# Group and instance sums through TensorE in pairs, maxima by a diagonal, the frame on GpSimd, and a new order of queues in a fused double convolution block

## The chip, the cores and the metric

The kernel runs on one core of one Trainium2 chip. The metric is the device time of one execution in microseconds; the median of three runs is taken. Five engines work side by side, each with an instruction queue of its own that runs strictly in order: TensorE (PE, matmuls), VectorE (DVE), ScalarE (ACT), GpSimd (POOL) and SyncE (SP), which here issues every transfer. They meet through semaphores. A queue whose first instruction waits holds back all that stands behind it.

## The reference, cut to what matters

The input x has the shape 8 x 32 x 128 x 128 (images, channels, rows, columns), fp32. Two residual blocks follow each other:

```python
x = x + _L0_conv_ref(_gn(x), L0_conv_weight, L0_conv_bias)
x = x + _L1_conv_ref(_gn(x), L1_conv_weight1, L1_conv_weight2)
```

`_gn` is a group norm with 16 groups of 2 channels, without weights. `_L0_conv_ref` rounds its input and its weights to integers from -127 to 127 (`q = round(t * 127 / max|t|)`, the maximum taken over the whole tensor of all images), convolves them 3x3, scales back and adds a bias. `_L1_conv_ref` is twice a convolution whose kernel is a weighted sum of fixed basis patterns, each followed by an instance norm and a leaky ReLU with slope 0.2:

```python
h = _instnorm_lrelu(_disco_conv(image, weight1))
return _instnorm_lrelu(_disco_conv(h, weight2))
```

At this size only five taps of that kernel are not zero: the centre and its four neighbours. Every norm needs a mean and a variance over pixels that lie on several partitions.

## The kernel before, in words

**Layout.** The 128 partitions are 4 bands of rows (quads) times 32 channels. An image in that layout is 128 x 4096 fp32, 2 MB. PSUM has 8 banks, used as two sets of four: every convolution of an image is done in two halves, g=0 into set 0 (banks 0 to 3) and g=1 into set 1 (banks 4 to 7). While one set is filled, the other is drained.

**Start.** All images are loaded one by one (`xa`), their group norms computed, the normalised x written out by GpSimd (`gn_x`, L658) and its absolute maximum taken by VectorE (`x_max`, L827). The maximum over the nine parts (L854) is taken over the partitions by GpSimd's `partition_all_reduce` (L673); L584 does the same for the weights. From it VectorE makes the factors of the rounding (L857 to L864, `quant_known`). `to_low` turns a piece of x (a quarter of an image) into int16 (ScalarE L530, GpSimd L691), `to_q` turns that into fp16 in the padded tile `qpad` or `c2one` (VectorE L874 for images 0 and 1, GpSimd L698 for the others).

**Three convolutions.** `quantised(b)`, v=0 (L1025), is the 3x3 convolution in fp16; VectorE adds its result to x plus bias (`x1_add`, L883) in the tile `x1_of(b)`, one of five (`LIVE`). `half(1, b, g)` (L1062) is half of the first five-tap convolution in fp32, with weights that `scale_taps` has multiplied by the norm's factor, and with a frame round the image that holds the mean (`frame`, L798 to L801), so that the norm need not be applied to the data. ScalarE copies it from PSUM to `hpad` (`take(1, t, g, n)`, L503) and applies norm and ReLU there in three steps (`make_h`, L516). `half(2, t, g)` is the second five-tap convolution, taken by ScalarE to `c2one` or `slot(4)` (`take(2, t, g, n)`), then normed in four pieces (`norm_out`, L524), added to x1 (`output`, GpSimd L704, VectorE L918 for the last two images) and stored. Each of the convolutions needs the rows of neighbouring partitions, which SyncE copies (`q_edges`, `x1_edges`, `h_edges`).

**The order.** `ORDER` sets TensorE's: after three opening entries the loop over t=0 to 5 runs `quantised(t+2)`, conv 1 of image t+1 and conv 2 of image t; then conv 1 of image 7 and conv 2 of images 6 and 7. A half may start when both pairs of banks of its set have been taken (`wait_set`). Each other engine has its own hand-written list over t, so all waits below come from these lists. `load_xb(b)` fetches x again for the addition, in four pieces of 0.5 MB, and `add_bias(b)` (ScalarE, L509) waits for all four (`xb_in`).

**Statistics.** VectorE reads each bank (`conv_stats`, L903) or the rows of x1 (`x1_stats`, L893) and joins them to one mean and variance per partition (`own_stat`). To sum over the partitions of a group or channel there are two ways. By DRAM: SyncE writes 128 x 2 numbers (`write_share`, L381), waits, and reads them back spread (`read_share`, L388 and L391). By TensorE: VectorE multiplies the numbers by a mask (`spread`), one small matmul with a matrix of zeros and ones sums them (`gather`, L979; for x L1082), and VectorE reads PSUM. `BY_PE` names the three cases of 24 that go by TensorE; `GATHERS` says after which tap the gather stands. `group_moments` (L789) makes the moments from either, and GpSimd makes scale and shift from them (`scale_of`, L619 and L622; `normalise`, L628; `scale_taps`, L638).

## Time and profile before

| what | us |
|---|---|
| median of 3 runs | 432.95 |
| lowest and highest | 431.23, 433.69 |
| the profiled execution | 430.53 |
| its span | 428.7 |
| busy: TensorE, VectorE, ScalarE, GpSimd | 258.9, 249.6, 214.2, 183.9 |
| TensorE's mean granted clock, of full speed | 0.908 |

The profile is of one execution. Busy times are sums of an engine's records. The chain of waits is followed back from the last instruction to whatever released it, and so says what set the end; "issue" in it is time in which the engine waited for nothing that the profile shows. In all rows PE is TensorE, DVE VectorE, ACT ScalarE, POOL GpSimd and SPq the queue of SyncE; L12 is line 12 of the program.

### The profile page before, as it was taken

The page shows a single profiled execution, that of the slowest core. Times are in us where ns is not written, and L with a number is a line of the kernel's source. Part 1 is how long each engine was busy: PE and PEld are TensorE (multiplying, and loading weights), DVE is VectorE, ACT ScalarE, POOL GpSimd, SP SyncE. Part 2 cuts the span into 40 slices and gives each one's busy share as a digit, 9 for nine tenths or more (in the row PEclk, how much of TensorE's full clock was granted, in tenths as well). Part 3 has the DMA queues.
Part 4 walks back from the last instruction along what each step waited for, and adds up shares of the span by engine and source line. Part 5 has one row for each costly group of instructions (what it writes and reads, how often), then busy time and mean ns, then how long its engine had stood idle before and what let it go on. Part 6 is the DMA issues. An engine that isn't in the chain of part 4 may idle for free.

```text
span 428.7 us, 14659 instructions
## 1 busy us (share of the span) xinstructions
PE 258.9 (60%) x6718; PEld 138.9 (32%) x6718; DVE 249.6 (58%) x418; ACT 214.2 (50%) x189; POOL 183.9 (43%) x220
## 2 busy tenths in 40 slices
PE   0011010373877977896896697459885994979700
PEld 0000000321443542462443253124442551655500
DVE  1838998169739717934860771348616853553264
ACT  1089981630321645492546440915474461676453
POOL 0298963196100905564824650638244063081000
PEclk9999999998898996998999699678996999798955
DMA  8999309602811906343824395328353141333066
GB/s 262 395 426 405 148 1 241 151 6 72 215 12 31 225 6 167 82 112 85 221 55 100 102 283 171 100 62 235 63 101 100 33 126 12 103 116 96 2 196 196
DMA packets 96513, 59.11 MB, mean 138 GB/s; under 512 B 20164, under 2 KB 95268, under 8 KB 95268
## 3 DMA queue, kind: packets, MB, share of 16 engines
q1 hardware_dynamic: 96452, 58.19, 47.7%
q8 instruction: 52, 0.85, 1.0%
q14 instruction: 9, 0.07, 0.1%
HBM read 36.41 MB, written 16.80 MB: 124 GB/s over the span
## 4 chain that ended last, share of the span: by engine, by line
DMA 33%; DVE 24%; POOL 15%; PE 9%; issue 7%; SPq 6%; ACT 5%; DVEq 0%; POOLq 0%; ACTq 0%
DMA stat_c<-own_stat_c 10%; DMA share_c<-stat_c 9%; DMA stat_x<-own_stat_x 9%; DVE amax L827 7%; PE ring L1062 6%; DVE bn_c L903 6%; SPq L388 3%; DVE bn_x L893 3%; DMA hpad<-w_dram 2%; ACT hpad L516 2%; DVE live L883 2%; DMA share_x<-stat_x 2%; POOL hpad L691 2%; POOL xs L691 2%; POOL qpad L698 2%
## 5 line engine op out<-in xcount | busy, mean ns | idle before, releaser
L1062 PE MATMUL ring<-hpad,w12t 32*32 32x512 f32 x2560 | 98.3, 619 | 16.2 <-ACT hpad L503 8.8
L903 DVE BATCH_NORM_STATS2 bn_c<-ring 128x6 f32<-128x512 f32 x128 | 79.1, 681 | 32.4 <-PE ring L1062 32.2
L1025 PE MATMUL ring<-qpad,w0t 64*32 64x512 f16 x1344 | 54.4, 488 | 39.4 <-ACT c2one L503 16.9
L1062 PEld LDWEIGHTS ring<-hpad,w12t 32*32 32x32 f32 x2560 | 54.8, 104 | 53.0 <-issue 28.6
L1062 PE MATMUL ring<-xs,w1s 32*32 32x512 f32 x1280 | 48.7, 632 | 8.9 <-ACT xs L503 5.3
L503 ACT COPY hpad<-ring 128x1024 f32<-128x1024 f32 x32 | 31.7, 1010 | 42.3 <-DVE bn_c L903 42.1
L619 POOL TENSOR_SCALAR var_eps<-moments_c 128x1 f32<-128x1 f32 x16 | 3.0, 191 | 107.8 <-DVE moments_c L789 107.8
L1062 PE MATMUL ring<-live,w1s 32*32 32x512 f32 x1280 | 46.4, 597 | 3.1 <-issue 3.1
L1025 PEld LDWEIGHTS ring<-qpad,w0t 64*32 64x32 f16 x1344 | 21.9, 114 | 74.2 <-ACT c2one L503 20.4
L789 DVE BATCH_NORM_AGGREGATE moments_x<-share_x 128x2 f32<-128x24 f32 x7 | 1.8, 264 | 66.6 <-DMA share_x<-stat_x 66.6
L516 ACT ACTIVATE hpad<-hpad,params 128x1536 f32<-128x1536 f32 (+1 forms) x24 | 35.0, 1523 | 10.2 <-POOL params L628 10.2
L1062 PEld LDWEIGHTS ring<-xs,w1s 32*32 32x32 f32 x1280 | 25.8, 105 | 30.6 <-issue 16.1
L503 ACT COPY xs<-ring 128x1024 f32<-128x1024 f32 x16 | 16.2, 1015 | 37.7 <-DVE bn_c L903 37.7
L503 ACT COPY c2one<-ring 128x1024 f32<-128x1024 f32 x16 | 16.3, 1020 | 32.6 <-DVE bn_c L903 32.5
L619 POOL TENSOR_SCALAR var_eps<-moments_x 128x1 f32<-128x1 f32 x8 | 2.0, 251 | 70.0 <-DVE moments_x L789 70.0
L1062 PEld LDWEIGHTS ring<-live,w1s 32*32 32x32 f32 x1280 | 24.4, 103 | 23.2 <-issue 14.5
L509 ACT ACTIVATE xs<-xs,single 128x1024 f32<-128x1024 f32 x16 | 17.1, 1146 | 25.4 <-DMA xs<-xb_dram 25.4
L691 POOL TENSOR_SCALAR xs<-xs,q_scale,q_shift 128x1024 int16<-128x1024 f32 x22 | 26.3, 1195 | 1.8
L524 ACT ACTIVATE c2one<-c2one,params 128x1024 f32<-128x1024 f32 x16 | 18.6, 1231 | 15.5 <-POOL params L628 15.5
L827 DVE TENSOR_REDUCE amax<-live 128x1 f32<-128x4096 f32 x5 | 22.0, 4393 | 6.9 <-POOL live L658 6.9
L460 ACT ACTIVATE qpad<-xs 128x4096 f16<-128x4096 f32 x4 | 14.4, 3608 | 17.4 <-DMA xs<-xa_dram 17.4
L883 DVE SCALAR_TENSOR_TENSOR live<-ring,single,live 128x512 f32<-128x512 f32 x32 | 21.5, 739 | 2.5 <-PE ring L1025 2.5
(107 smaller groups left out, 383.5 us busy)
## 6 DMA issues: line engine op xcount, KB each, us to landing
xs<-xa_dram SPq DMA_DIRECT2D x8, 2048.0 KB, 10.4
live<-xb_dram SPq DMA_DIRECT2D x16, 512.0 KB, 6.9
xs<-xb_dram SPq DMA_DIRECT2D x16, 512.0 KB, 7.0
out_dram<-live SPq DMA_DIRECT2D x16, 512.0 KB, 4.9
out_dram<-xs SPq DMA_DIRECT2D x16, 512.0 KB, 5.1
hpad<-xa_dram SPq DMA_DIRECT2D x1, 2048.0 KB, 8.4
live<-live SPq DMA_DIRECT2D x8, 192.0 KB, 2.8
xs<-xs SPq DMA_DIRECT2D x8, 192.0 KB, 3.2
```

The lines of the kernel that those rows point to most:

```text
L388: sp.dma_start(share[s][f:P:2, :, 1:3], of.unsqueeze(0).to_broadcast([QUADS, C // 2, GN_MEMBERS, 2])).then_inc(shared[s], 16)
L460: nc.scalar.activation(junk, grid(x_first(b)), ACT.Identity, scale=1.0 / (SUM_ROOT * COLS), accum_out=own_x[:, b, 1:2]).then_inc(x_meaned, 1)
L503: nc.scalar.copy(to, pair_of(g, n)).then_inc(taken[v], 1)
L509: nc.scalar.activation(x, x, ACT.Identity, bias=bias[:]).then_inc(biased, 1)
L516: nc.scalar.activation(rows, rows, ACT.Prelu, bias=param(shift["c1"], t), scale=param(scale["c1"], t), alpha=SLOPE).then_inc(h_ready, 1)
L524: nc.scalar.activation(y, y, ACT.Prelu, bias=param(shift["c2"], t), scale=param(scale["c2"], t), alpha=SLOPE).then_inc(out_norm, 1)
L691: nc.gpsimd.tensor_scalar(low_of(b, n), piece(source, n), q_scale[:, b:b + 1], q_shift[:, b:b + 1], ALU.mult, ALU.add).then_inc(low_pool, 1)
L827: nc.vector.tensor_reduce(amax[:, n:n + 1], gn_tile(b)[:, c0:c1], AX.X, ALU.max, apply_absolute_value=True).then_inc(max_done, 1)
L883: ins = nc.vector.scalar_tensor_tensor(x, grid(ring[:, bank_of(g, 2 * i + p), :]), dequant[:], x, ALU.mult, ALU.add)
L903: ins = nc.vector.bn_stats(bn[f"c{v}"][:, QUADS * g + k, :], ring[:, bank_of(g, k), :])
L1025: ins = nc.tensor.matmul(ring[C * c:C * (c + 1), bank_of(g, 2 * i + p), :].rearrange("p (y x) -> p y x", x=IMG), w0t[q, tap, :], q_of(b)[q ...
L1062: ins = nc.tensor.matmul(ring[C * c:C * (c + 1), bank_of(g, r), :].rearrange("p (y x) -> p y x", x=IMG), w, window(v, b, r, c, g, dy, dx), ...
```

## The change

What it does:

- The sums of x1 for all images and of c1 (the first five-tap convolution) for all images go by TensorE. For images in the loop, x1(t+2) and c1(t+1) are gathered in one stop, after the third tap of `half(2, t, 1)`, into a bank of set 0. In the title's words "second convolution" is this one: the quantised one is the first. Of c2 the last two images go by TensorE; images 0 to 5 stay with DRAM.
- Both maxima over the partitions are taken by a diagonal: VectorE multiplies an identity matrix (loaded from DRAM as a new input) by the 128 maxima, TensorE multiplies by a matrix of ones, and VectorE reduces the row in PSUM. `qmul` falls away, its factor is joined into the next step.
- `frame` moves from VectorE to GpSimd, behind `scale_taps`.
- In the conversions before the loop ScalarE makes two pieces of image 0 and two of image 1, GpSimd the rest; `add_bias(0)` stands ahead of them.
- The lists of SyncE, ScalarE, GpSimd and VectorE are put in another order. `load_xb(t+3)` and `add_bias(t+3)` are split in two for t from 1 to 4 and stand earlier; in the tail some outputs change engine.

The order on SyncE in iteration t=2, before:

```order
L372 DMA live<-xb_dram 128x8x128 [waits stored0]
L372 DMA live<-xb_dram 128x8x128 x3
L347 DMA hpad<-hpad 96x128 [waits h_ready]
L348 DMA hpad<-hpad 96x128
L381 DMA stat_c<-own_stat_c 4x32x2 [waits stat_step_c2]
L391 DMA share_c<-stat_c 128x4x2 [waits written_c2]
```

and after:

```order
L391 DMA stat_c<-own_stat_c 4x32x2 [waits stat_step_c2]
L386 DMA live<-xb_dram 128x8x128 [waits stored0]
L386 DMA live<-xb_dram 128x8x128
L395 DMA share_c<-stat_c 128x4x2 [waits written_c2]
L360 DMA hpad<-hpad 96x128 [waits h_ready]
L361 DMA hpad<-hpad 96x128
L386 DMA live<-xb_dram 128x8x128 [waits stored0]
L386 DMA live<-xb_dram 128x8x128
```

The sums of c2 went ahead of the load, and the load is cut in two round `h_edges`; the two trips of x1 and c1 that stood later in the iteration are gone.

The order on ScalarE in iteration t=2, before (L516 is `make_h`, L503 a take, L524 `norm_out`, L509 `add_bias`):

```order
L516 ACTIVATE hpad<-hpad,params 128x4x2x128 [waits conv1_taken,norm_ready_c1]
L516 ACTIVATE hpad<-hpad,params 128x4x3x128 x2
L503 COPY hpad<-ring 128x2x4x128 [waits conv2_done,conv1_counted]
L503 COPY hpad<-ring 128x2x4x128 [waits conv1_counted]
L524 ACTIVATE xs<-xs,params 128x1024 [waits conv2_taken,norm_ready_c2]
L524 ACTIVATE xs<-xs,params 128x1024 x3
L503 COPY hpad<-ring 128x2x4x128 [waits conv1_counted] x2
L509 ACTIVATE live<-live,single 128x8x128 [waits xb_in5]
L509 ACTIVATE live<-live,single 128x8x128 x3
```

and after (the same in this order: L515, L502, L523, L508):

```order
L515 ACTIVATE hpad<-hpad,params 128x4x2x128 [waits conv1_taken,norm_ready_c1]
L515 ACTIVATE hpad<-hpad,params 128x4x3x128 x2
L508 ACTIVATE live<-live,single 128x8x128 [waits xb_in5]
L508 ACTIVATE live<-live,single 128x8x128
L502 COPY hpad<-ring 128x2x4x128 [waits conv2_done,conv1_counted]
L502 COPY hpad<-ring 128x2x4x128 [waits conv1_counted]
L508 ACTIVATE live<-live,single 128x8x128 [waits xb_in5]
L508 ACTIVATE live<-live,single 128x8x128
L523 ACTIVATE xs<-xs,params 128x1024 [waits conv2_taken,norm_ready_c2]
L502 COPY hpad<-ring 128x2x4x128 [waits conv1_counted] x2
L523 ACTIVATE xs<-xs,params 128x1024 x3
```

`add_bias`, with its wait for the load, moved from the end of the row to right behind `make_h`, ahead of the takes.

The order on GpSimd where the maximum of x is taken, before:

```order
L658 TENSOR_SCALAR c2one<-hpad,gn_scale,gn_shift 128x2048 [waits max_done,norm_ready_x]
L673 ISA
L673 ISA single<-single 128x1 [waits amax_step]
L676 MEMSET c2one 128x2x130 [waits max_done]
L677 MEMSET c2one 128x32x2
L691 ISA
L691 TENSOR_SCALAR hpad<-xs,q_scale,q_shift 128x1024 [waits quant_known]
```

and after:

```order
L681 TENSOR_SCALAR c2one<-hpad,gn_scale,gn_shift 128x2048 [waits max_done,norm_ready_x]
L696 MEMSET c2one 128x2x130 [waits max_done]
L697 MEMSET c2one 128x32x2
L711 TENSOR_SCALAR hpad<-xs,q_scale,q_shift 128x1024 [waits quant_known]
L711 TENSOR_SCALAR hpad<-xs,q_scale,q_shift 128x1024 x3
```

The all-reduce and both plain ISA rows round it are gone.

In the diff, cut to its core, a line of "..." marks what is left out:

```diff
+GATHERS = {(0, 1, 0): (6, [("x1", 0)]), (1, 0, 1): (3, [("x1", 1)]), (1, 1, 0): (4, [("c1", 0)]),
+           (2, B - 2, 0): (4, [("c1", B - 1)]), (2, B - 1, 0): (4, [("c2", B - 2)])}
+for _t in range(B - 2):
+    GATHERS[2, _t, 1] = (3, [("x1", _t + 2), ("c1", _t + 1)])
+LAST_GATHER = ("c2", B - 1)
...
             for t in range(B - 2):
+                if t >= 1:
+                    write_share(t - 1)
+                if t >= 1 and t + 3 < B:
+                    load_xb(t + 3, (0, 1))
+                if t >= 1:
+                    read_share(t - 1)
+                h_edges(t)
+                if t >= 1 and t + 3 < B:
+                    load_xb(t + 3, (2, 3))
+                x1_edges(t + 2)
...
+            add_bias(0)
 
             act.wait_ge(quant_known, 1)
...
                 for n in range(3):
                     make_h(t, n)
+                if t >= 1 and t + 3 < B:
+                    add_bias(t + 3, (0, 1))
                 take(1, t + 1, 0, 0)
                 take(1, t + 1, 0, 1)
+                if t >= 1 and t + 3 < B:
+                    add_bias(t + 3, (2, 3))
                 if t >= 1:
-                    for n in range(QUADS):
-                        norm_out(t - 1, n)
+                    norm_out(t - 1, 0)
                 take(1, t + 1, 1, 0)
                 take(1, t + 1, 1, 1)
-                if t + 3 < B:
-                    add_bias(t + 3)
+                if t >= 1:
+                    for n in range(1, QUADS):
+                        norm_out(t - 1, n)
...
-            pool.wait_ge(amax_step, 1)
-            nc.gpsimd.partition_all_reduce(sx[:], amax1[:], P, ABSMAX).then_inc(sx_done, 1)
...
+            def max_of_all(all_of, of, n, bank):
+
+                nc.vector.tensor_scalar(diagonal, eye, of, None, ALU.mult).then_inc(max_diagonal, 1)
+                dve.wait_ge(max_shared, n + 1)
+                return nc.vector.tensor_reduce(all_of, ring[:, bank, 0:P], AX.X, ALU.max)
...
             own_of("x1", 0)
-            x1_add(1, 0)
             group_moments("x1", 0)
-            frame(0)
...
                 conv_stats(1, t + 1, 1)
+                conv_stats(2, t, 0)
                 group_moments("x1", b)
-                frame(b)
-                conv_stats(2, t, 0)
                 group_moments("c1", t + 1)
...
+            def share_max(n, bank):
+                pe.wait_ge(max_diagonal, n + 1)
+                nc.tensor.matmul(ring[:, bank, 0:P], ones, diagonal, start=True, stop=True).then_inc(max_shared, 1)
```

## Rows read from the trace of the kernel before

**Rows 1.** The page: busy time, then the chain by line.

```profile
PE 258.9 (60%) x6718; PEld 138.9 (32%) x6718; DVE 249.6 (58%) x418; ACT 214.2 (50%) x189; POOL 183.9 (43%) x220
...
DMA stat_c<-own_stat_c 10%; DMA share_c<-stat_c 9%; DMA stat_x<-own_stat_x 9%; DVE amax L827 7%; PE ring L1062 6%; DVE bn_c L903 6%; SPq L388 3%; DVE bn_x L893 3%; DMA hpad<-w_dram 2%; ACT hpad L516 2%; DVE live L883 2%; DMA share_x<-stat_x 2%; POOL hpad L691 2%; POOL xs L691 2%; POOL qpad L698 2%
```

**Rows 2.** Chain of waits at the start: start us, length us, what.

```profile
12.97 4.80 issue
...
40.99 0.61 PE ring L1082 x2
...
74.59 2.59 issue
...
78.52 6.08 issue
```

**Rows 3.** The same chain inside iterations t=2 and t=3.

```profile
205.46 4.38 ACT hpad L516 x3
...
225.76 5.74 DMA stat_x<-own_stat_x
...
233.74 4.27 DMA stat_c<-own_stat_c
```

**Rows 4.** Groups of instructions: out<-in, shapes, xcount, busy us, mean ns, idle before.

```profile
L903 DVE BATCH_NORM_STATS2 bn_c<-ring 128x6 f32<-128x512 f32 x128 | 79.1, 681 | 32.4 <-PE ring L1062 32.2
...
L503 ACT COPY hpad<-ring 128x1024 f32<-128x1024 f32 x32 | 31.7, 1010 | 42.3 <-DVE bn_c L903 42.1
...
L883 DVE SCALAR_TENSOR_TENSOR live<-ring,single,live 128x512 f32<-128x512 f32 x32 | 21.5, 739 | 2.5 <-PE ring L1025 2.5
...
L524 ACT ACTIVATE c2one<-c2one,params 128x1024 f32<-128x1024 f32 x16 | 18.6, 1231 | 15.5 <-POOL params L628 15.5
L704 POOL TENSOR_TENSOR xs<-xs,c2one 128x1024 f32<-128x1024 f32 x8 | 17.3, 2178 | 2.7 <-ACT c2one L524 2.7
...
L509 ACT ACTIVATE live<-live,single 128x1024 f32<-128x1024 f32 x16 | 17.0, 1142 | 0.0
...
L798 DVE TENSOR_SCALAR live<-zeros,moments_x 128x64 f32<-128x64 f32 x4 | 1.1, 284 | 0.1
```

**Rows 5.** Timeline of TensorE: start us, length us, instruction, xcount, idle before.

```profile
87.98 1.48 PE L1025 MATMUL ring<-qpad,w0t 64*32 64x512 f16 x24 [8.83 <-DVE qpad L874]
...
123.22 2.80 PE L1025 MATMUL ring<-qpad,w0t 64*32 64x512 f16 x95
...
163.36 8.04 PE L1025 MATMUL ring<-qpad,w0t 64*32 64x512 f16 x192 [4.86 <-ACT c2one L503]
...
326.64 8.30 PE L1025 MATMUL ring<-qpad,w0t 64*32 64x512 f16 x192 [5.87 <-ACT c2one L503]
...
364.27 12.99 PE L1062 MATMUL ring<-xs,w1s 32*32 32x512 f32 x311 [5.32 <-ACT xs L503]
```

**Rows 6.** Stretches: busy (xcount) by engine, then PEclk, DMA share, GB/s.

```profile
228.30:234.00 5.70, 5.55 (x160) 2.88 (x160) 0.00 (x0) 4.11 (x4) 1.28 (x1) 1.00 0.48 95
...
274.00:281.50 7.50, 7.27 (x160) 3.43 (x160) 0.00 (x0) 4.23 (x5) 1.39 (x1) 0.74 0.34 74
```

**Rows 7.** Timeline of SyncE's queue, iteration t=2.

```profile
204.97 4.14 SPq L372 DMA_DIRECT2D live<-xb_dram  x4
```

**Rows 8.** The line of load_xb, and the page's issues of stores.

```profile
DMA to landing us min/median/max: 4.3/7.0/9.4
...
out_dram<-live SPq DMA_DIRECT2D x16, 512.0 KB, 4.9
```

**Rows 9.** Waits of TensorE: us in total, times, longest.

```profile
PE ring L1062 <- issue: 10.5, 14, 1.6
```

**Rows 10.** Chain of waits in the tail.

```profile
396.72 3.84 DMA stat_c<-own_stat_c
...
400.57 3.56 DMA share_c<-stat_c
...
418.15 3.50 DVE xs L918 x3
```

More of the change, by code:

```diff
@@ L154, in slot @@
             return xs[:, n * COLS:(n + 1) * COLS]
+        eye, ones, diagonal = (flat(hpad[0])[:, n * P:(n + 1) * P] for n in range(3))
         last_x = flat(hpad[1])[:, 0:COLS]
@@ L308, in low_pool_count @@
         def low_pool_count(b, n):
-            return 2 + 4 * (b - 1) + n
+            return 4 + 4 * (b - 2) + n
         def shares(s, n):
-            return sum((s, m) not in BY_PE for m in range(n + 1))
+            return sum((s, m) not in GATHER_SET for m in range(n + 1))
         block = ctx.enter_context(nc.Block())
@@ L525, in norm_out @@
                                      alpha=SLOPE).then_inc(out_norm, 1)
+            add_bias(0)
             act.wait_ge(quant_known, 1)
-            for n in (0, 1):
-                nc.scalar.activation(low_of(0, n), piece(x_first(0), n), ACT.Identity,
-                                     bias=q_shift[:, 0:1], scale=q_scale[:, 0:1]).then_inc(low_act, 1)
-            add_bias(0)
+            for b in range(2):
+                for n in (0, 1):
+                    nc.scalar.activation(low_of(b, n), piece(x_first(b), n), ACT.Identity,
+                                         bias=q_shift[:, b:b + 1], scale=q_scale[:, b:b + 1]).then_inc(low_act, 1)
             add_bias(1)
@@ L561, in _ @@
             take(1, z, 0, 1)
-            for n in range(QUADS):
+            for n in range(2):
                 norm_out(t - 1, n)
@@ L565, in _ @@
             take(1, z, 1, 1)
-            take(2, t, 0, 0)
             for n in range(3):
                 make_h(z, n)
+            take(2, t, 0, 0)
             take(2, t, 0, 1)
+            for n in range(2, QUADS):
+                norm_out(t - 1, n)
             for n in range(2):
                 take(2, t, 1, n)
+            for n in range(QUADS):
+                norm_out(t, n)
             take(2, z, 0, 0)
             take(2, z, 0, 1)
-            for n in range(QUADS):
-                norm_out(t, n)
             take(2, z, 1, 0)
@@ L708, in _ @@
             pool.wait_ge(quant_known, 1)
[L709 to L712 removed]
+            for b in range(2):
+                for n in (3, 2):
+                    to_low(b, n)
+            for n in range(4):
+                to_low(2, n)
             pool.wait_ge(q_dve, 4)
@@ L716, in _ @@
             zero_bands(hpad[1]).then_inc(h_border, 1)
-            for n in range(4):
-                to_low(2, n)
-            for n in range(4):
-                to_q(2, n)
+            to_q(2, 0)
+            to_q(2, 1)
             scale_taps(0)
-            scale_taps(1)
-            normalise("c1", 0)
+            frame(0)
+            to_q(2, 2)
+            to_q(2, 3)
             for t in range(B - 2):
+                scale_taps(t + 1)
+                frame(t + 1)
+                normalise("c1", t)
                 if t + 3 < B:
@@ L731, in _ @@
                     normalise("c2", t - 1)
[L732 removed]
+                    for n in range(QUADS):
                         output(t - 1, n)
[L734 to L743 removed]
+            t, z = B - 2, B - 1
+            scale_taps(z)
+            frame(z)
+            normalise("c1", t)
+            normalise("c2", t - 1)
+            output(t - 1, 0)
+            output(t - 1, 1)
+            normalise("c1", z)
+            output(t - 1, 2)
+            output(t - 1, 3)
+            normalise("c2", t)
+            output(t, 2)
+            output(t, 3)
+            normalise("c2", z)
         @block.vector
@@ L927, in _ @@
             own_of("x1", 0)
-            x1_add(1, 0)
             group_moments("x1", 0)
-            frame(0)
-            x1_add(1, 1)
+            for g in range(2):
+                x1_add(1, g)
             for g in range(2):
@@ L962, in _ @@
             conv_stats(1, z, 1)
+            group_moments("c1", z)
             conv_stats(2, t, 0)
-            group_moments("c1", z)
             conv_stats(2, t, 1)
+            group_moments("c2", t)
             conv_stats(2, z, 0)
-            group_moments("c2", t)
-            for n in range(QUADS):
-                output(t, n)
+            output(t, 0)
+            output(t, 1)
             conv_stats(2, z, 1)
```

263 lines of the change are left out of this document (120 added, 143 removed).

## The prediction

> **What bounds the kernel now.** I read the chain of waits first: no engine is busy more than 60% of the span, and the largest links of the chain are not arithmetic but transfers of a few hundred sums to DRAM and back [rows 1]. Then the same chain inside one iteration of the loop over t: a write of x1's sums takes 5.74 us, c1's write 4.27, with a read behind each, all issued by SyncE in one row, and only behind them come conv statistics, `make_h` and the next convolution [rows 3]. Then TensorE's own timeline: `quantised(3)` starts at 163.36, `quantised(7)` at 326.64, the last `half(1, 7)` at 364.27 [rows 5]. So four iterations take 163.3 us, 40.8 each, and the next 37.6. What must TensorE itself do in one? Half of a fp32 convolution of 160 records takes 5.55 us at a granted clock of 1.00 [rows 6], `quantised` 2.80 for one of its two halves [rows 5]: 4 x 5.55 + 2 x 2.80 = 27.8 us. 13 us of each iteration are waits. The start is the third view: between the maximum over all (DVE L854) and the first conversion on GpSimd lie 2.59 us, the all-reduce, and 6.08 us in which GpSimd waits for nothing the profile shows; a similar hole of 4.80 us follows the first all-reduce [rows 2].
>
> **The change part by part.** Times below are against the profiled execution (span 428.7).
>
> *Maxima.* One all-reduce goes; in its place stand a `tensor_scalar` of 128x128, one matmul of 128x128 and a `tensor_reduce` from PSUM. The nearest matmul pair over 128 partitions took 0.61 us [rows 2]; three small VectorE steps at 0.28 [rows 4] and the hand-overs make about 1.5 us, between 1.1 and 2.5. Two scalar steps fall out before `quant_known`. 74.59 + 1.5 + 0.6 gives `quant_known` at 76.7, against 78.5. The holes of 6.08 and 4.80 us: in the instruction order an ISA row stands at L673 and another at L691, right where the 6.08 us lie, and likewise at L584 and L593; in the new order both pairs are gone but for one at the very start. I take the 6.08 as gone (bounds 0 and 6.1). The early 4.80 is worth less, since later sums on ScalarE and the loads of x pace that stretch: 2.9 us, less 0.4 us for one more load in front: 2.5 (bounds 0 and 4.8). Now the cover: `add_bias(0)` stands ahead of ScalarE's conversions. Its four pieces take 4 x 1.14 [rows 4]; its load lands about 7 us after the issue [rows 8], before `quant_known`, so it costs about nothing (up to 1 us if it lands late). The conversions of image 1 are split over ScalarE and GpSimd. The last cast of image 0, and with it TensorE's first matmul at 87.98 [rows 5], comes at about 78.6: **9.4 us** gained.
>
> *Order at the start.* `group_moments("x1", 0)` now stands ahead of `x1_add(1, 0)`, 4 adds of 0.67 [rows 4]: 1.9 us. The moments of x1(1) stood behind a round trip by DRAM; now they come inside `half(1, 0, 1)`, and VectorE's next statistics no longer queue behind the transfer: 4.4 us at `quantised(2)`. Iteration t=0 then needs 2.8 (rest of `quantised`), two convolutions, 1.3 where the takes stand behind `make_h`, and the pauses below: 28.4 against 32.5, 4.1 us. Sum 9.4 + 1.9 + 4.4 + 4.1 = **19.8**: `quantised(3)` starts at 143.6.
>
> *Pair of gathers.* x1(t+2) and c1(t+1) are summed in one stop after tap 3 of `half(2, t, 1)`: two matmul pairs of 0.61, in all 0.7 to 1.3 us on TensorE per iteration. The gather waits for the spreads (VectorE, about 2 us earlier) and for `take(2, t, 0, 0)`, since it writes into that bank. Behind it stand two taps of the convolution and everything else of TensorE. The moments follow about 1.8 us later, just as the convolution ends, so `quantised(t+3)` loses at most 0.3.
>
> *Frame on GpSimd.* On VectorE the three fills cost 0.28 each [rows 4], and VectorE is no bound, so their leaving gains nothing by itself. On GpSimd I take 1.1 us with their mutual waits; the trace has no such fill on GpSimd, and an add of 1024 columns takes 2.18 there [rows 4], so 0.8 to 6.5 for the three. `scale_taps` (1.4) and `frame` end 2.3 us after `quantised` starts; `half(1, t+1)` needs them 5.6 after it. Hidden, with 3.3 us to spare, except before `half(1, 7)`, where no `quantised` stands between: 1.1 us there.
>
> *Loads and ScalarE.* Here lies the new wait, and it decides the sum. Count from T, the start of `quantised(t+2)`, t from 1 to 4. VectorE has c2's aggregate at T+3.0, SyncE writes it, and issues two pieces of `load_xb(t+3)`, for which the last store of t-2 must have landed, 4.9 us after its issue [rows 8], near T. `read_share` comes at 7.7, `h_edges` until 9.9, then the other two pieces at about 1.03 each [rows 7], the last one at 10.9. A piece lands 4.3 to 7.0 us after issue [rows 8]; with two in a row I take 5: T+16. But `add_bias(t+3, (0, 1))` waits for all four (`xb_in` at 64) and stands on ScalarE ahead of `take(1, t+1, 0)`. ScalarE is ready for it at T+8 (takes until 3.65, then `make_h` of 4.38 [rows 3]). So: add_bias 16.0 to 18.3, two takes of 1.01 [rows 4] to 20.4, while TensorE, finished with `half(1, t+1)` at 16.9, waits 3.5 us for them. Then two pieces to 22.7, one `norm_out` of 1.23 to 23.9, two takes to 26.0, three `norm_out` to 29.7, `take(2, t, 0, 0)` at 30.75: only now may the gather run. TensorE started `half(2, t, 0)` at 20.4; whether the idle time lowers its clock (a half took 7.27 at 0.74 and 5.55 at 1.00 [rows 6]) doesn't matter, as the gather waits for 30.75 anyway. Two gathers and two taps: 30.75 + 0.7 + 2.2 = 33.7. A second loop gives the same: `norm_out` of piece 3 feeds GpSimd's add of 2.18, the store, its landing, the loads: 33.8. To this I add TensorE's pauses with no releaser, 10.5 us in 16 fp32 convolutions [rows 9], 0.65 each, 1.3 per iteration: **35.0 us**, 4 x 35.0 = 140 against 163.3, **23.3** gained. With a piece that lands in 4.3 us the iteration is 34.3, in 7.0 it is 37.
>
> *Iteration t=5* has no load: 27.8, gathers 0.7, hand-overs 1.5, pauses 1.3 and the wait for the frame 1.1: 32.4 against 37.6, **5.2**.
>
> *Tail.* From `half(1, 7, 0)`: 11.1, then four taps of `half(2, 6, 0)` and the gather of c1(7), moments at 16.4; GpSimd 1.1, `make_h` 4.4, `take(2, 6, 0)` 2.0: `half(2, 7, 0)` starts at 24.0, ends 29.7, its second half 35.3; statistics, spread, gather, moments 4.1; GpSimd 1.1; first `norm_out` 1.25 and four adds (three took 3.50 [rows 10]) 46.7; store and close 6: 53, with pauses 54.3, against 428.7 - 364.3 = 64.4: **10.1**. The round trip of c2(6), 3.84 + 3.56 [rows 10], is the bulk of it. VectorE adds two pieces of image 6 while GpSimd adds others. The Trainium skill (SBUF — State Buffer, on the shared port pair) says that a VectorE instruction with two SBUF inputs blocks against a GpSimd one that reads SBUF; by it one such add may wait 2.18, and with 0.9 us of slack ahead of the last statistics the tail would be 1.3 longer. No row of before has the two side by side; my sum leaves it out.
>
> Sum: 19.8 + 23.3 + 5.2 + 10.1 = 58.4, span 370.3. Around the span lie 1.8 us, and the median is 2.4 above the profiled execution: 370.3 + 1.8 + 2.4 = **375**.
>
> **The rivals.** *A: the iteration doesn't shorten.* The store, load, `add_bias`, take, `norm_out` loop has so much jitter (landings up to 9.4 [rows 8], an issue of SyncE ahead of each) that iterations 1 to 4 stay at 40.8. Only start and end gain: 375 + 23 = 398. For it: two loops of equal length meet in one queue. Against: it needs a landing at T+22.
>
> *B: TensorE bound.* If the loads land before ScalarE asks (T+8), the iteration is 30: 375 - 20 = 355. Against: two pieces are issued only after 9.9. For it: if SyncE issues two pieces quicker than four in a row and TensorE's clock stays up, part of this comes true.
>
> *C: the hole of 6.08 us stays*, because it isn't the all-reduce that brings it, and the change doesn't do there what it says: 375 + 6 = 381, inside the range.
>
> *D: slower.* TensorE is held in its queue at the pair of gathers by ScalarE, which is held by a load. This decides from the point at which the five iterations give back the 35 us of start and tail and 2 more: 7.5 us over 40, hence a gather at T+44 and a landing at T+30 in every iteration. 35.0 + 13 = 48 each, 375 + 5 x 13 = 440. The nearest row is the slowest landing, 9.4, which is far from it.
>
> **How the numbers follow.** Forecast with its bounds (start gains 14 to 22, iteration 34 to 37, tail 8 to 12), C within it: 0.70, 366 to 388. A and what lies between, 388 to 400: 0.14. B in part or whole, 354 to 366: 0.12. D 0.02; the rest, a gain that almost vanishes, 0.02. The range 358 to 400 leaves out part of B, D and the rest. Faster by over 0.5% (about what a measurement of this kernel can tell from no change) 0.96, within it 0.02, slower 0.02.
>
> **What would show it.** Right: no hole on GpSimd after `quant_known`; x1 and c1 sums gone from the chain; `quantised` at 35 us intervals; ScalarE waiting some 8 us for the xb load after `make_h`, TensorE waiting for `hpad` takes before `half(2, t, 0)`. Wrong: an interval near 30 with ScalarE never waiting for a load (B), or near 40 (A); a hole that stays (C).

## The result, and the profile after

The changed kernel takes 397.79 us (median of four runs, 394.1 to 398.43) against 432.09 us of the kernel before, measured again beside it: a ratio of 0.9187 [0.912, 0.9253]. The forecast was 375.0 with a range from 358 to 400. So the sign and the range held, and the forecast itself was 23 us too low. The profiled execution has a span of 396.6 us against a predicted 370.3. Where a median doesn't answer exactly to its ratio below, the ratio leaves out runs that were disturbed.

The page of the kernel after: busy times, the chain by engine and by line, and the two groups of `add_bias`.

```profile
PE 254.8 (64%) x6752; PEld 138.1 (35%) x6752; DVE 252.6 (64%) x407; ACT 214.7 (54%) x191; POOL 194.8 (49%) x242
...
DMA 26%; PE 18%; DVE 16%; ACT 15%; SPq 10%; POOL 8%; issue 4%; DVEq 0%; POOLq 0%; ACTq 0%
PE ring L1086 14%; DMA xs<-xb_dram 8%; DMA xs<-xa_dram 8%; DMA live<-xb_dram 6%; DVE amax L851 5%; POOL live L724 4%; DVE bn_c L929 4%; SPq L386 4%; SPq L360 3%; ACT hpad L502 3%; ACT xs L508 3%; DMA stat_c<-own_stat_c 2%; PE ring L1049 2%;
...
L508 ACT ACTIVATE xs<-xs,single 128x1024 f32<-128x1024 f32 x16 | 17.3, 1141 | 56.7 <-DMA xs<-xb_dram 56.7
...
L508 ACT ACTIVATE live<-live,single 128x1024 f32<-128x1024 f32 x16 | 17.3, 1144 | 28.1 <-DMA live<-xb_dram 28.1
```

Beside [rows 1] and [rows 4]: TensorE, VectorE and ScalarE do about the work they did before, GpSimd 11 us more. The other group of `add_bias` in the kernel before has one wait, at the start:

```profile
L509 ACT ACTIVATE xs<-xs,single 128x1024 f32<-128x1024 f32 x16 | 17.1, 1146 | 25.4 <-DMA xs<-xb_dram 25.4
```

So ScalarE never waited in front of `add_bias` in the loop over t, and now it waits 84.8 us in front of it in all: 27.7 at the start, where the kernel before waited 25.4, and 57.1 in the loop. Transfers still hold 26% of the chain, but other ones: 14% are the loads of x for the addition, 2% are left of the writes of c2's sums.

TensorE's timeline, to set beside [rows 5]: the starts of the `quantised` convolutions from image 0 on, then `half(1, 7, 0)`; between them the longest wait of an iteration and the longest pause.

```profile
81.25 1.48 PE L1049 MATMUL ring<-qpad,w0t 64*32 64x512 f16 x24 [2.35 <-DVE qpad L900]
...
117.27 5.41 PE L1049 MATMUL ring<-qpad,w0t 64*32 64x512 f16 x192
...
156.92 5.42 PE L1049 MATMUL ring<-qpad,w0t 64*32 64x512 f16 x192
...
183.24 10.45 PE L1086 MATMUL ring<-hpad,w12t 32*32 32x512 f32 x256 [7.72 <-ACT hpad L502]
...
210.18 8.21 PE L1086 MATMUL ring<-xs,w1s 32*32 32x512 f32 x185 [3.10 <-issue]
...
231.78 5.71 PE L1049 MATMUL ring<-qpad,w0t 64*32 64x512 f16 x192
...
271.00 5.41 PE L1049 MATMUL ring<-qpad,w0t 64*32 64x512 f16 x192
...
308.15 5.62 PE L1049 MATMUL ring<-qpad,w0t 64*32 64x512 f16 x192
...
341.40 4.44 PE L1086 MATMUL ring<-xs,w1s 32*32 32x512 f32 x65 [3.49 <-POOL xs L660]
```

`quantised(4)` starts at 196.44, in the same timeline. From these starts come the stages of the sum:

| stage | predicted | measured | off |
|---|---|---|---|
| `quantised(3)` starts | 143.6 | 156.92 | +13.3 |
| iterations t=1 to 4 | 140 | 39.5 + 35.3 + 39.2 + 37.1 = 151.2 | +11.2 |
| iteration t=5 | 32.4 | 33.25 | +0.85 |
| tail from `half(1, 7, 0)` | 54.3 | 55.2 | +0.9 |

ScalarE in iteration t=1 (T, the start of `quantised(t+2)`, is 156.92), which shows the mechanism:

```profile
160.59 4.38 ACT L515 ACTIVATE hpad<-hpad,params 128x1024 f32<-128x1024 f32 x3
179.18 2.19 ACT L508 ACTIVATE xs<-xs,single 128x1024 f32<-128x1024 f32 x2 [14.21 <-DMA xs<-xb_dram]
181.28 1.91 ACT L502 COPY hpad<-ring 128x1024 f32<-128x1024 f32 x2
```

It finishes `make_h` at 164.97, as forecast at T+8, and then waits 14.21 us for the load. TensorE stands behind the two takes (7.72 us, above). The chain of waits of the same iteration says what makes the load late:

```profile
160.07 4.74 DMA stat_c<-own_stat_c
164.83 1.35 SPq L395
...
166.22 4.66 SPq L360
170.93 0.60 SPq L361
...
171.57 0.58 SPq L386
172.19 6.97 DMA xs<-xb_dram
```

In iterations t=2, 3 and 4 the issue of `h_edges` (L360) took 1.85, 3.56 and 1.74 us, the landing of the last piece 7.87, 7.25 and 7.72.

### The profile page after: what moved, and what is told of

It is laid out like the page before. It is cut to its first block, busy times and chain, and to the rows that moved or that the text cites. A ratio compares the mean times of both kernels' runs of the same rounds, so it can differ in the third digit from the quotient of the medians.

```text
span 396.6 us, 14732 instructions
## 1 busy us (share of the span) xinstructions
PE 254.8 (64%) x6752; PEld 138.1 (35%) x6752; DVE 252.6 (64%) x407; ACT 214.7 (54%) x191; POOL 194.8 (49%) x242
## 4 chain that ended last, share of the span: by engine, by line
DMA 26%; PE 18%; DVE 16%; ACT 15%; SPq 10%; POOL 8%; issue 4%; DVEq 0%; POOLq 0%; ACTq 0%
PE ring L1086 14%; DMA xs<-xb_dram 8%; DMA xs<-xa_dram 8%; DMA live<-xb_dram 6%; DVE amax L851 5%; POOL live L724 4%; DVE bn_c L929 4%; SPq L386 4%; SPq L360 3%; ACT hpad L502 3%; ACT xs L508 3%; DMA stat_c<-own_stat_c 2%; PE ring L1049 2%; ACT hpad L515 2%; ACT live L508 2%
## 5 line engine op out<-in xcount | busy, mean ns | idle before, releaser
L1086 PE MATMUL ring<-hpad,w12t 32*32 32x512 f32 x2560 | 97.7, 640 | 22.2 <-ACT hpad L502 19.9
L1086 PEld LDWEIGHTS ring<-hpad,w12t 32*32 32x32 f32 x2560 | 51.7, 107 | 59.2 <-ACT hpad L502 25.7
L1086 PE MATMUL ring<-xs,w1s 32*32 32x512 f32 x1280 | 49.8, 653 | 9.7 <-issue 5.5
L1086 PE MATMUL ring<-live,w1s 32*32 32x512 f32 x1280 | 45.6, 599 | 5.7 <-issue 5.0
L508 ACT ACTIVATE xs<-xs,single 128x1024 f32<-128x1024 f32 x16 | 17.3, 1141 | 56.7 <-DMA xs<-xb_dram 56.7
L1049 PE MATMUL ring<-qpad,w0t 64*32 64x512 f16 x1344 | 40.8, 393 | 4.3 <-DVE qpad L900 2.4
L515 ACT ACTIVATE hpad<-hpad,params 128x1536 f32<-128x1536 f32 (+1 forms) x24 | 35.0, 1523 | 13.9 <-POOL params L633 13.9
L502 ACT COPY hpad<-ring 128x1024 f32<-128x1024 f32 x32 | 31.3, 1011 | 19.0 <-DVE bn_c L929 19.0
L1086 PEld LDWEIGHTS ring<-xs,w1s 32*32 32x32 f32 x1280 | 25.9, 107 | 32.2 <-issue 24.5
L508 ACT ACTIVATE live<-live,single 128x1024 f32<-128x1024 f32 x16 | 17.3, 1144 | 28.1 <-DMA live<-xb_dram 28.1
L1086 PEld LDWEIGHTS ring<-live,w1s 32*32 32x32 f32 x1280 | 23.6, 103 | 24.6 <-issue 14.5
L1049 PEld LDWEIGHTS ring<-qpad,w0t 64*32 64x32 f16 x1344 | 19.3, 95 | 27.7 <-issue 8.3
L624 POOL TENSOR_SCALAR var_eps<-moments_c 128x1 f32<-128x1 f32 x16 | 3.1, 192 | 50.6 <-DVE moments_c L826 49.9
L724 POOL TENSOR_TENSOR xs<-xs,c2one 128x1024 f32<-128x1024 f32 x8 | 17.3, 2191 | 19.0 <-ACT c2one L523 19.0
L724 POOL TENSOR_TENSOR live<-live,xs 128x1024 f32<-128x1024 f32 x8 | 17.4, 2195 | 16.8 <-ACT xs L523 16.8
L459 ACT ACTIVATE qpad<-xs 128x4096 f16<-128x4096 f32 x4 | 14.4, 3609 | 19.7 <-DMA xs<-xa_dram 19.7
L502 ACT COPY c2one<-ring 128x1024 f32<-128x1024 f32 x16 | 15.7, 1010 | 13.1 <-DVE bn_c L929 13.0
L502 ACT COPY xs<-ring 128x1024 f32<-128x1024 f32 x16 | 15.8, 1012 | 12.8 <-DVE bn_c L929 12.8
L718 POOL TENSOR_SCALAR qpad<-xs 128x1024 f16<-128x1024 int16 x22 | 22.5, 1053 | 0.1
```

The lines of the kernel that those rows point to most:

```text
L502: nc.scalar.copy(to, pair_of(g, n)).then_inc(taken[v], 1)
L508: nc.scalar.activation(x, x, ACT.Identity, bias=bias[:]).then_inc(biased, 1)
L515: nc.scalar.activation(rows, rows, ACT.Prelu, bias=param(shift["c1"], t), scale=param(scale["c1"], t), alpha=SLOPE).then_inc(h_ready, 1)
L718: nc.gpsimd.tensor_scalar(bands(qpad)[:, n * CHUNK:(n + 1) * CHUNK, :], grid(low_of(b, n)), 1.0, 0.0, ALU.mult, ALU.add).then_inc(q_pool, 1)
L724: nc.gpsimd.tensor_tensor(x, x, grid(piece(c2_of(t), n)), ALU.add).then_inc(out_pool, 1)
L1049: ins = nc.tensor.matmul(ring[C * c:C * (c + 1), bank_of(g, 2 * i + p), :].rearrange("p (y x) -> p y x", x=IMG), w0t[q, tap, :], q_of(b)[q ...
```

## The experiments

The theory (H in the expectations): ScalarE, and through it TensorE, is held by `add_bias(t+3, (0, 1))`, which waits for all four pieces although it needs two. The rivals: the iterations are long because of TensorE's pauses or because of the landings themselves, in whatever order; and for the start, that conversions and not the order of loads make it late. Numbers of different chips are compared by their ratio to the kernel before on the same chip.

**The changed kernel once more, as a yardstick.**

> The changed kernel itself, on the chip on which the next kernels run, as their yardstick: a ratio of 0.919 to the kernel before, as measured for it, whatever the chip's own level. Its iterations t=0 to 4 again near 39.6, 39.5, 35.3, 39.2 and 37.2 us.

It took 396.79 us, ratio 0.9165 [0.9107, 0.9223]. Its iterations t=0 to 5 were 39.1, 39.5, 34.3, 40.6, 34.7 and 35.2 us.

**A semaphore for each two pieces.**

```diff
-                                 ).then_inc(xb_in[b], 16)
+                                 ).then_inc(xb_in[b] if m < 2 else xb_in_late[b], 16)
...
-                act.wait_ge(xb_in[b], 16 * QUADS)
+                if 0 in of:
+                    act.wait_ge(xb_in[b], 32)
+                if 2 in of:
+                    act.wait_ge(xb_in_late[b], 32)
```

> Two semaphores for each xb load: the first add_bias of an iteration waits for its own two pieces only, the second for the other two. Theory H (the changed kernel's iterations are set by ScalarE, which waits for all four pieces ahead of the takes; TensorE then waits at the pair of gathers): add_bias of two pieces (2.2 us) and two takes (1.9) leave the chain behind the landing, so iterations t=1 to 4 fall from 37.8 us on average to about 33.8; 16 us less, 382. Rival R (the waits for the load are slack, and the loop of output, store and load or TensorE's own speed sets the iteration): within 3 us of 398.

It took 383.14 us, ratio 0.8753 [0.8696, 0.881], (0.9165 - 0.8753) x 439 = 18 us less than the changed kernel on that measure; the changed kernel itself did not run on that chip. ScalarE in iteration t=2:

```profile
193.51 4.38 ACT L519 ACTIVATE hpad<-hpad,params 128x1024 f32<-128x1024 f32 x3 [0.72 <-POOL params L637]
201.83 2.19 ACT L512 ACTIVATE live<-live,single 128x1024 f32<-128x1024 f32 x2 [3.94 <-DMA live<-xb_dram]
```

The wait is 3.94 us where it was 11.06; over the four iterations ScalarE's waits for loads, those for the second two pieces included, come to 33.6 us where they were 49.9. Iterations t=1 to 4 come to 137.7 us against 151.2 in the changed kernel (149.1 in its repetition); t=0, whose load is not cut, stays at 39.0. So the trace shows 11 to 13 us of the 18. The wait for pieces that the next two steps don't need is shown to set the length of these iterations. It doesn't explain why they were longer than forecast, since the forecast had this wait in its sum.

**The four pieces in one row, ahead of the read of c2's sums and of `h_edges`.**

```diff
-                    load_xb(t + 3, (0, 1))
+                    load_xb(t + 3)
...
-                if t >= 1 and t + 3 < B:
-                    load_xb(t + 3, (2, 3))
```

> All four pieces of load_xb(t+3) are issued in one row, ahead of the read of c2's sums and of h_edges. H: the last piece lands some 6 us sooner (it no longer stands behind the wait for the write of c2's sums, 4.7 us, and behind h_edges), so each of the iterations t=1 to 4 is 5 to 6 us shorter, 376. R: within 3 us of 398, or longer, since h_edges and the sums of c2 come 2 us later.

385.56 us, ratio 0.8787 [0.8727, 0.8847]. The direction is right, the size is not: 376 was expected. Iterations t=1 to 4 took 33.9, 34.5, 36.6 and 33.2. What stands between the two halves of the load (the read of the sums and `h_edges`) is worth about 13 us in all.

**Short loads.** Images 5 to 7 are loaded with one row in eight, so their outputs are not the reference's; the number of transfers is the same.

```diff
+                    rows = CHUNK if b < LIVE else 1
-                    sp.dma_start(inner(x1_of(b))[:, n], grid(xb_d[b, :, n * PIECE:(n + 1) * PIECE])
+                    sp.dma_start(inner(x1_of(b))[:, n, 0:rows], grid(xb_d[b, :, n * PIECE:n * PIECE + rows * IMG])
```

> The loads of images 5, 6 and 7 bring one row in eight of each piece (the rest of the tile keeps older values, so these images' outputs are not the reference's); issue order and waits are the same. H: the last piece lands about 2.5 us after its issue in place of 7.3, in three iterations, so 3 x 4.8 = 14 us less, 384. R: within 3 us of 398.

376.7 us, ratio 0.8581 [0.8531, 0.8632], 7 us below the expected 384. Iterations t=2 to 4 took 29.1, 31.3 and 29.8: with the load out of the way the period is the 30 us of rival B. Iteration t=1, with a full load, took 40.4. Waits of TensorE in the whole run (in us, how often, the longest):

```profile
PE ring L1087 <- ACT hpad L503: 11.4, 3, 9.6
PE ring L1087 <- issue: 6.5, 6, 2.0
```

In the kernel after these rows read 19.9 and 11.6. The second row, TensorE's pauses without a releaser, scatters too much to read an effect of the fewer bytes from it: with full loads it reads 10.6 in the repetition of the changed kernel, and between 8.2 and 16.4 in the other runs.

**The load of image 3 ahead of everything else in iteration t=0.** In the kernel after SyncE and ScalarE did this (two timelines of one kernel, SyncE's rows first):

```profile
130.87 0.53 SPq L360 DMA_DIRECT2D hpad<-hpad  x1
...
136.04 4.63 SPq L386 DMA_DIRECT2D xs<-xb_dram  x4
...
147.37 4.26 ACT L508 ACTIVATE xs<-xs,single 128x1024 f32<-128x1024 f32 x4 [7.22 <-DMA xs<-xb_dram]
```

The load stands behind `h_edges`, which waits until 130.87 for `make_h`, though its tile is free long before.

```diff
+                if t == 0:
+                    load_xb(3)
                 if t >= 1:
                     write_share(t - 1)
...
-                if t == 0:
-                    load_xb(3)
```

> load_xb(3) stands first in iteration t=0 on SyncE, ahead of h_edges(0), whose wait holds the queue until 130.9, in place of behind x1_edges(2). H: iteration t=0 is long (39.6 us from quantised(2) to quantised(3), where my sum had 31) because add_bias(3) waits on ScalarE until 147.4 for a load issued at 136, and TensorE waits at the pair of gathers for the take behind it; with the load landed by 125 the iteration is 31 to 32: 8 us less than the control. Rival (iteration t=0 is long by its own work: the statistics of two images and c1's norm behind TensorE): within 2 us of the control.

389.31 us, ratio 0.8906 [0.8840, 0.8972]: less than the yardstick by (0.9165 - 0.8906) x 433 = 11.2 us by the ratios and by 7.5 by the medians, where 8 were expected. Iteration t=0 took 30.8 us instead of 39.1, and ScalarE, in its timeline, no longer waits there:

```profile
141.30 4.27 ACT L508 ACTIVATE xs<-xs,single 128x1024 f32<-128x1024 f32 x4
```

**All three edits of the loads together.**

> The three edits together: load_xb(3) first, all pieces in one row ahead of the sums of c2, and one semaphore for each two pieces. H: ScalarE waits for a load at most 1 to 2 us in an iteration, iterations t=0 to 4 at 31 to 33 us, 30 to 36 us less than the control: 362 to 368. If another wait takes over at once (GpSimd's four adds, or TensorE's pauses without a releaser, which sum to 14.2 us in the kernel with two semaphores): 370 to 378, with iterations at 34.

369.71 us, ratio 0.8514 [0.8456, 0.8573], and on another chip, beside later runs, 373.65 us and 0.8415 [0.8346, 0.8483]. It leaves nothing of the computation out. The iterations are 31.3, 32.2, 33.4, 32.5, 33.1 and 32.8. What is left in them shows in one iteration (T = 181.55), SyncE, ScalarE, TensorE:

```profile
185.65 7.03 SPq L387 DMA_DIRECT2D live<-xb_dram  x4
...
194.53 2.19 ACT L510 ACTIVATE live<-live,single 128x1024 f32<-128x1024 f32 x2 [3.87 <-DMA live<-xb_dram]
...
195.98 7.62 PE L1088 MATMUL ring<-xs,w1s 32*32 32x512 f32 x177 [3.89 <-issue]
```

That is at the border of the two outcomes expected, and the rows speak for the second: other waits take a part. ScalarE's waits for a load in the loop are down to 3.9 to 6.5 us each, 20.6 in all where they were 57.1, and not to the 1 to 2 us of the first outcome. TensorE's pauses without a releaser come to 12.1 us, and to 16.4 in the repetition.

**The frame back on VectorE, behind both moments** (`frame` is taken from GpSimd's list; the three fills follow `group_moments` of x1 and c1 on VectorE).

```diff
-                frame(t + 1)
...
                 group_moments("x1", b)
                 group_moments("c1", t + 1)
+                frame(b)
```

> The frame goes back to VectorE, behind both moments; all else as changed. GpSimd's fills took 0.37 each, VectorE's 0.28. If the frame is hidden behind quantised in all iterations as I worked out, only half(1, 7), which has no quantised ahead of it, gains about 1 us: within 2 us of the control. If it isn't (GpSimd is what ends last before half(1, t+1)): 5 us less or more.

A miss: 391.56 us, ratio 0.9054 [0.9008, 0.9099], 5 us less than the yardstick. TensorE's wait before `half(1, 7, 0)` went from 3.5 to

```profile
337.08 3.40 PE L1080 MATMUL ring<-xs,w1s 32*32 32x512 f32 x98 [2.12 <-POOL w1s L642]
```

and that accounts for 1.4 us. TensorE's pauses without a releaser came to 8.2 us where the yardstick had 10.6. The rest doesn't sit in one place in the trace. So the frame was tried again on top of the three edits, beside their repetition, and with `scale_taps(7)` one output addition earlier:

> The kernel with the three edits of the loads together once more, unchanged, as the yardstick on the same chip for the three kernels beside it: 366 to 371 us, ratio to before 0.845 to 0.857.

> The three edits of the loads, and the frame back on VectorE. Theory F (the frame on GpSimd has a price where no quantised convolution hides it): TensorE's wait of 3.5 us before half(1, 7) shrinks to about 2.1, and the tail by about 1.4 more, so 2 to 4 us less than the yardstick beside it, 365 to 368 us. Theory N (the 5 us of the earlier run lay in the landings of the loads, not in the frame): within 1 us of the yardstick, and the iterations t=1 to 4 don't differ.

> As the kernel before it, and GpSimd scales the weights of image 7 one output addition (2.18 us) earlier. If GpSimd's row of output additions is what holds half(1, 7), the wait before it falls from about 2.1 to under 0.5 us and the time by another 1.5 to 2 us; if it is the gather's moments on VectorE, by less than 0.5.

The medians are 373.65, 371.15 and 372.41 us. The ratios are 0.8415 [0.8346, 0.8483] for the repetition, 0.844 [0.8391, 0.8488] with the frame on VectorE, 0.8458 [0.8427, 0.849] with the earlier taps too. The three can't be told apart. Before `half(1, 7, 0)` both edits do what was expected; in TensorE's timeline it waits 2.12 us in the second, and in the third not at all, but the 1.5 to 2 us that this was to save don't show in the time:

```profile
311.51 2.35 PE L1083 MATMUL ring<-hpad,w12t 32*32 32x512 f32 x64
313.89 9.85 PE L1083 MATMUL ring<-xs,w1s 32*32 32x512 f32 x299
```

The 2 us are smaller than what the iterations before scatter by (30.9 to 37.2 in the repetition). What gave 5 us in the first run with the frame stays open; it didn't return.

**The all-reduce back for the maximum of x**, first on the changed kernel, then on the three edits.

```diff
+            pool.wait_ge(amax_step, 1)
+            nc.gpsimd.partition_all_reduce(sx[:], amax1[:], P, bass.bass_isa.ReduceOp.absmax).then_inc(sx_done, 1)
...
-            max_of_all(sx[:], amax1[:], 1, MAX_BANKS["x"]).then_inc(sx_done, 1)
...
-            share_max(1, MAX_BANKS["x"])
+            pe.wait_ge(amax_step, 1)
```

> The maximum of x over the partitions goes by GpSimd's all-reduce again, as in the kernel before; all else as changed. If the hole of 6.08 us on GpSimd belongs to the all-reduce: a hole of about 6 us comes back, quant_known is 1 to 2 us later, and the time is 6 to 8 us longer, 405. If the hole had gone for another reason: 1 to 2 us longer, 399.5. If the waits for the loads of xb swallow the delay: less than 2 us although the hole is back.

400.2 us, ratio 0.9116 [0.9057, 0.9175]. There was no yardstick on that chip, and the ratio is within that of the changed kernel, so the time says nothing; the trace has the hole back, and `quantised(0)` starts at 86.02 instead of 81.25. Hence the second try, with a yardstick:

> The three edits of the loads, with GpSimd's all-reduce back for the maximum of x, the frame left on GpSimd. Theory H (the all-reduce brings a hole of about 6 us on GpSimd that delays the first conversions, and nothing behind it wins the time back): quantised(0) starts about 4.8 us later than in the yardstick and the time is 4 to 6 us longer. Theory C (the hole is covered, ScalarE's conversions and add_bias(0) set the start): under 1.5 us longer.

377.06 us, ratio 0.8587 [0.8524, 0.8651] against 0.8415 [0.8346, 0.8483]: by the ratios 0.0172 x 440.3 = 7.6 us, by the medians 3.4. GpSimd in this kernel:

```profile
73.89 0.41 POOL L698 PARTITION_ALL_REDUCE single<-single  x1 [6.59 <-issue]
74.18 0.38 POOL L701 MEMSET c2one<- 128x260 f16 x1
...
81.77 6.07 POOL L716 TENSOR_SCALAR hpad<-xs,q_scale,q_shift 128x1024 int16<-128x1024 f32 x4 [6.99 <-issue]
```

and in the repetition of the three edits beside it:

```profile
74.22 0.31 POOL L698 MEMSET c2one<- 128x260 f16 x1 [5.29 <-DVE amax L853]
74.48 0.28 POOL L699 MEMSET c2one<- 128x64 f16 x1
76.78 5.84 POOL L713 TENSOR_SCALAR hpad<-xs,q_scale,q_shift 128x1024 int16<-128x1024 f32 x4 [2.02 <-DVE q_shift L887]
```

The factors are known 2.3 to 2.4 us after VectorE's last own maximum by either way; the gain lies in the 6.99 us hole behind. `quantised(0)` starts at 85.14 and 81.44, 3.7 us apart. But VectorE's last own maximum ended earlier in the kernel with the all-reduce, at 72.73 against 74.36. Counted from there it is 12.4 us against 7.1, so 5.3 us of the hole are paid, near the 4.8 of the expectation. No run takes the sums of x1 and c1 back to DRAM or the list orders back one by one, so what each of these parts gives by itself is read from traces here and not measured.

## Why the prediction was right and where it was wrong

**Maxima: right in its main term.** The hole of 6.08 us [rows 2] is gone: GpSimd's first conversion starts at 76.61 behind `q_shift`, as in the rows of the repetition above, and with the all-reduce back the hole is back too. Rival C (the hole stays) is out. The diagonal took VectorE 0.44, TensorE 0.76 and VectorE 0.29, with hand-overs 1.7 us against 1.5 taken. Wrong was the *early hole* of 4.80 us, put at 2.5. VectorE's last own maximum ends at 74.19 instead of 74.58, so it was worth 0.4 (0.2 to 2.0 in the other kernels without it): the loads of x and VectorE's reductions set that stretch. The cover of `add_bias(0)` held nearly. Its load landed at 73.23, ScalarE began to convert at 77.43, 0.8 us after GpSimd. In all 6.7 us were gained at `quantised(0)` and not 9.4. The 9.4 itself isn't the sum of its terms: 1.8 at `quant_known`, 6.1 and 2.5 make 10.4, and the text doesn't say what takes 1.0 off.

**Order at the start: right up to iteration t=0, then the largest single miss.** From the start of `quantised(0)` to the end of `quantised(2)` it took 47.4 us before and 41.4 after, so 6.0 gained where 1.9 + 4.4 were forecast. Its end was still 4.7 us later than in the forecast (122.7 against 143.6 - 25.6 = 118.0): 2.65 from `quantised(0)`, and most of the rest because I took its second half at 2.8 us, where before it had taken 4.5. From there to `quantised(3)` the forecast was 28.4 - 2.8 = 25.6 us and the run took 34.2. The step that failed is "Iteration t=0 then needs 2.8 ..., two convolutions, 1.3 ..., and the pauses": it put the wait for the load of image 3 at nothing, though this load has no early place in SyncE's list in t=0 and ScalarE waited 7.22 us for it. (The terms that it names make 27.6, or 28.3 with a pair of gathers, and not 28.4.) With that load moved forward the iteration fell from 39.1 to 30.8. The view for it was there: the list of SyncE in t=0 had to be walked as that of t=2 was.

**Loads and ScalarE: the mechanism right, the last landing put too early.** The wait named is the wait that came. Landings were forecast at T+16 and came at T+22.3, T+19.1, T+21.7 and T+20.1, in sum 19.1 us later. From the landing to the next T the forecast was 17.7 us; measured were 17.3, 16.2, 17.6 and 17.1, 2.7 less in sum. TensorE's pauses, added at 1.3 for each iteration, mostly fell inside the wait for the load and cost nothing more: 5.2 less. 19.1 - 2.7 - 5.2 = 11.2 us, the whole miss of these iterations. Both parts of "the last one at 10.9 ... I take 5" were at fault, to equal shares. The landing took 7.0 to 7.9 us, in sum 9.8 more. The rows gave 4.3 to 7.0 [rows 8] as bounds, and with two of four pieces just behind another two, and the edges, the middle wasn't the likeliest value; the value for 7.0 stood in the text as 37 us for an iteration, close to the 37.8 measured. And the last issue began at T+15.3, 11.2, 14.4 and 12.3, in sum 9.6 late. For the most part this is the first issue of `h_edges`, which took 4.66, 1.85, 3.56 and 1.74 us behind the first two pieces, against 0.53 us with no load ahead of it (iteration t=0 above); in t=3 the issue of one piece took 3.63 us besides. Bytes in flight aren't all there is to it: in the kernel before, behind four pieces, it took 0.64 to 1.75 us.

From the landing to the next T the length was right, and in part by luck. The forecast had the gather wait for `take(2, t, 0, 0)` at T+30.75 and said that TensorE's clock doesn't matter. In t=1, 3 and 4 the gather followed TensorE's own matmuls without a wait. Stretches of `half(2, t)` up to the gather, in t=2 behind a short wait and in t=3 behind 7.27 us of idle time (busy time and count by engine, granted clock, DMA share, GB/s):

```profile
219.63:228.30 8.67, 8.67 (x256) 4.95 (x256) 4.32 (x9) 8.67 (x9) 4.66 (x3) 1.00 0.21 62
257.48:268.10 10.62, 10.62 (x256) 6.15 (x256) 2.49 (x4) 9.87 (x10) 6.61 (x4) 0.79 0.43 141
```

The same 256 records took 8.67 us at a clock of 1.00 and 10.62 at 0.79. Two takes, these 10.6 and the last taps happen to be as long as ScalarE's row in the forecast.

**Rival A's number, not its mechanism.** 398 is the time that rival A gave, with iterations t=1 to 4 at 40.8. They did shorten, to 37.8, and the rest of the miss is the start. Half of A is true: the landing came near the T+22 that it needs, in t=1 and t=3. The chance of 0.14 for 388 to 400 was too low for a forecast whose largest unknown, the landing, had 7.0 us as the median of one row.

**Rival B** is what short loads show: 29 to 31 us for an iteration. There the load's wait stands in front of it. **Rival D** is far off, in no iteration did the gather come later than T+36.7.

**Pair of gathers: right.** They take 0.4 us each, overlapping, and moments are there 1.5 to 1.9 us before the convolution ends. Chains of x1 and c1 by DRAM [rows 3] are gone, of c2 one remains with 4.74 us.

**Frame on GpSimd: right for `half(1, t+1)` in the loop, blind to `make_h`, too small at the end.** The fills take 0.37 us each and 1.5 with hand-overs, where 1.1 was taken. No `half(1, t+1)` of the loop waits for them. But the norm of c1 stands behind them in GpSimd's row, and `make_h` waits for that norm, in iteration t=3:

```profile
236.53 4.37 ACT L515 ACTIVATE hpad<-hpad,params 128x1024 f32<-128x1024 f32 x3 [1.10 <-POOL params L633]
```

In the kernel with the three edits it waits 0.70 to 1.10 us in each iteration from t=2 to 5, and with the frame on VectorE in none of them. The times don't show it (0.8415 and 0.844 above). Before `half(1, 7, 0)` TensorE waits 3.49 us. GpSimd's timeline tells why: the output additions of image 4 stand ahead of it.

```profile
331.88 6.48 POOL L724 TENSOR_TENSOR xs<-xs,c2one 128x1024 f32<-128x1024 f32 x3 [4.70 <-ACT c2one L523]
338.46 0.19 POOL L624 TENSOR_SCALAR var_eps<-moments_x 128x1 f32<-128x1 f32 x1
```

The moments were there at 336.0. The forecast priced the fills and not the row of instructions ahead of them.

**Tail: right within 0.9 us.** Its terms up to the four adds make 46.4 and not 46.7. The 1.3 us that the Trainium skill's rule would have added are nearly there, by other instructions than the adds. VectorE's multiplication of sums by the mask, `spread_c`, with GpSimd idle, then beside an addition on GpSimd (VectorE's rows are those of L937):

```profile
330.06 0.17 DVE L937 TENSOR_TENSOR spread_c<-const,own_stat_c 128x12 f32<-128x12 f32 x1
...
354.84 4.33 POOL L724 TENSOR_TENSOR live<-live,xs 128x1024 f32<-128x1024 f32 x2 [1.36 <-ACT xs L523]
...
357.82 1.37 DVE L937 TENSOR_TENSOR spread_c<-const,own_stat_c 128x12 f32<-128x12 f32 x1
```

The long one ends at 359.19, GpSimd's addition at 359.17, and it lies on the chain: 1.2 us. The statistics from PSUM beside the same additions keep their 0.62 us each. The Trainium skill (SBUF — State Buffer, SBUF: two separate sides) says that of the two whichever starts first holds the shared ports for its whole instruction, where the VectorE one has two SBUF inputs. The trace agrees, down to the end of the wait. Another such wait, 2.09 us for `spread_x` at 325.13, lies on the chain of iteration t=5. And the prediction's "No row of before has the two side by side" holds only for adds of whole pieces; the kernel before had a `spread_c` of 1.54 us beside GpSimd's additions, also on its chain (GpSimd's row, then VectorE's):

```profile
377.85 6.47 POOL L704 TENSOR_TENSOR live<-live,xs 128x1024 f32<-128x1024 f32 x3 [1.36 <-ACT xs L524]
...
380.67 1.54 DVE L911 TENSOR_TENSOR spread_c<-const,own_stat_c 128x12 f32<-128x12 f32 x1
```

## What to carry to other kernels

When a transfer is cut in parts to be used earlier, cut the semaphore too: a wait for the whole, placed ahead of work that TensorE needs, cost 11 to 18 us here, and three small edits of where loads are issued and waited for took the ratio from 0.9165 to 0.8514, three quarters of what the large change had given. Walk the list of the issuing queue in every iteration that differs, the first one above all. And where a forecast hangs on the landing of a load, take the slow end of the row that shows loads of that size, and count the issues that stand behind bulk transfers as longer than they are alone.
